# The last chunk's dispatch of an expert-routed transformer kernel: two groups of four row transfers, or four groups of two

## The reference

```
h_flat = (style-modulated norm of x).reshape(2048, 256)
probs = softmax(h_flat @ router_w)            # 8 experts
gates, idx = top_k(probs, 2); gates /= gates.sum(-1)
hid  = relu(h_flat @ exp_w1[e] + exp_b1[e])   # 256 -> 1024
eout = hid @ exp_w2[e] + exp_b2[e]            # 1024 -> 256
out  = x + sum over the two experts of gate * eout
```

## Time and profile before

| | us |
|---|---|
| runs, median of 3 (lowest to highest) | 653.52 (652.57 to 654.47) |
| profiled execution, its own time | 655.13 |
| its span | 653.3 |
| granted TensorE clock, mean | 0.949 |
| TensorE busy | 585.7 |
| VectorE busy | 458.3 |
| ScalarE busy | 308.5 |
| POOL busy | 223.4 |

### The profile page before, as it was taken

One profiled execution on the slowest core, in us unless ns is written; L12 is line 12 of the kernel. 1 busy time (PEld: TensorE's weight loads), 2 busy tenths in 40 slices (PEclk: granted clock), 3 DMA queues, 4 the chain that ended last, 5 costly groups with the idle time before them and its releaser, 6 DMA issues.

```text
span 653.3 us, 15487 instructions
## 1 busy us (share of the span) xinstructions
PE 585.7 (90%) x5008; PEld 422.1 (65%) x5008; DVE 458.3 (70%) x1282; ACT 308.5 (47%) x643; POOL 223.4 (34%) x137
## 2 busy tenths in 40 slices
PE   3979989899878999859987799999899999999995
PEld 1537575476665585844857447778677877777773
DVE  5755995789977879781898752988555656666663
ACT  2418446545373436564343241767456444444442
POOL 3140615047417067043380240222542223323123
PEclk9978899899997999979997699999899999999999
DMA  7995009513285450665605595774533222222320
GB/s 209 321 240 171 3 18 256 190 45 114 68 182 178 138 179 2 171 152 194 206 22 193 219 330 217 270 261 97 140 91 58 44 47 45 45 38 41 58 40 12
DMA packets 41189, 86.58 MB, mean 133 GB/s; under 512 B 7321, under 2 KB 31938, under 8 KB 37026
## 3 DMA queue, kind: packets, MB, share of 16 engines
q1 hardware_dynamic: 21248, 56.47, 25.3%
q0 software_dynamic: 8352, 16.99, 14.1%
q10 hardware_dynamic: 11522, 12.20, 6.2%
HBM read 57.10 MB, written 29.44 MB: 132 GB/s over the span
## 4 chain that ended last, share of the span: by engine, by line
PE 60%; DVE 19%; ACT 7%; DMA 5%; issue 5%; POOL 2%; ACTq 1%; another core or an unknown queue 1%; SPq 0%; POOLq 0%; DVEq 0%
PE bank L1959 10%; PE bank L1768 6%; PE bank L1948 6%; PE bank L1950 5%; PE bank L1949 5%; PE bank L1960 5%; PE bank L1777 4%; DMA stage<-in_moe_w 4%; PE bank L1667 3%; PE bank L1732 2%; PE bank L1748 2%; PE bank L1626 2%; ACT split L685 2%; DVE sc_sum L1155 2%; DVE stats L1075 1%
## 5 line engine op out<-in xcount | busy, mean ns | idle before, releaser
L1950 PE MATMUL bank<-xs_f,w_moe 128*128 128x128 f16 x624 | 122.9, 221 | 2.4 <-issue 2.4
L1948 PE MATMUL bank<-xs_f,w_moe 128*128 128x128 f16 x624 | 122.8, 221 | 2.0 <-DVE xs_f L1520 0.9
L1949 PE MATMUL bank<-xs_f,w_moe 128*128 128x128 f16 x624 | 122.4, 220 | 0.5 <-issue 0.5
L906 ACT ACTIVATE stage<-bank,cols 128x128 f32<-128x128 f32 x312 | 88.9, 370 | 62.7 <-PE bank L1950 26.9
L646 POOL DMA_INDIRECT out_x<-x_kept,ids x39 | 62.6, 1605 | 159.5 <-DVE x_kept L1534 117.8
L1948 PEld LDWEIGHTS bank<-xs_f,w_moe 128*128 x624 | 61.3, 98 | 37.3 <-issue 8.1
L1959 PE MATMUL bank<-w_moe,split 128*128 x208 | 79.5, 384 | 0.6
L1768 PE MATMUL bank<-w_moe 128*128 128x512 f32 x128 | 60.8, 636 | 5.3 <-ACT w_moe L755 5.3
L1042 DVE SCALAR_TENSOR_TENSOR split<-stage,split 128x2048 f16<-128x2048 f32 x16 | 40.2, 2514 | 35.7 <-ACT split L685 35.7
L1949 PEld LDWEIGHTS bank<-xs_f,w_moe 128*128 x624 | 61.5, 99 | 4.0 <-issue 0.9
L558 POOL TENSOR_TENSOR w_moe<-w_moe,sc_max 128x2048 f32<-128x2048 f32 x8 | 29.0, 3622 | 99.1 <-DVE sc_max L1150 99.1
(11 more groups left out here) (271 smaller groups left out, 1196.7 us busy)
## 6 DMA issues: line engine op xcount, KB each, us to landing
stage<-in_moe_w SPq DMA_DIRECT2D x16, 1024.0 KB, 7.9
w_split<-split SPq DMA_DIRECT2D x16, 1024.0 KB
w_moe<-w_split SPq DMA_DIRECT2D x8, 2048.0 KB
w_moe<-in_bias POOLq DMA_DIRECT2D x8, 1024.0 KB, 9.1
xs<-dispatched ACTq DMA_DIRECT2D x41, 130.0 KB
w_moe<-in_x_f SPq DMA_DIRECT2D x4, 512.0 KB, 7.2
w_moe<-in_x_t SPq DMA_DIRECT2D x4, 512.0 KB, 8.0
out_x<-x4b ACTq DMA_DIRECT2D x4, 512.0 KB
```

The costliest lines, as they stand in the source:

```text
L906: ins = act.activation(h32[j][:, f, :], bank[banks + g][:, P * (f % 4):P * (f % 4) + P], ACT.Relu, bias=moe_b1[:, bass.ds(e, 1), f], scale ...
L1948: pe.matmul(o, hi, xs_f[j][:, k, :], start=(k == 0), stop=False)
L1949: pe.matmul(o, hi, xs_f[j][:, KD + k, :], start=False, stop=False)
L1950: mm = pe.matmul(o, lo, xs_f[j][:, k, :], start=False, stop=(k == KD - 1))
```

## The change

POOL's order around the last chunk's dispatch is written anew. In place of transfers for groups 0 and 1, add 6, transfers for groups 2 and 3, add 7, and `confirm`, it runs the two transfers of one group and one add, four times (adds 6 to 9), and `confirm` behind the last add. The adds behind it start at 10 instead of 8. Buffers and semaphores of each add are the same as before (9's `i % 2` and `i % STEPS` give what n gave).

```diff
@@ -655,12 +655,11 @@
             pool.wait_ge(x_stored.sem, x_stored.of(NCH - 1, 0))
             for n in range(6):
                 add_rows(n, n % 2, n % STEPS)
-            dispatch(NCH - 1, range(0, 2))
-            add_rows(6, 0, 0)
-            dispatch(NCH - 1, range(2, TT))
-            add_rows(7, 1, 1)
+            for i in range(TT):
+                dispatch(NCH - 1, range(i, i + 1))
+                add_rows(6 + i, i % 2, i % STEPS)
             confirm(NCH)
-            for n in range(8, EARLY):
+            for n in range(6 + TT, EARLY):
                 add_rows(n, n % 2, n % STEPS)
             pool.wait_ge(x_stored.sem, x_stored.of(NCH, 0))
             with pool.Fori(0, TURNS - EARLY_TURNS) as i:
```

## The result

The changed kernel takes 656.70 us (median of 7 runs, 655.09 to 658.09), the kernel before 652.95 beside it: ratio 1.0054, 95% interval 1.0035 to 1.0073, **3.7 us slower** (2.3 to 4.8 by the interval). The forecast was +3.8.

A forecast was written before the change was run, and what follows sets the result against it. TensorE bounds the kernel, with 8.0 us lost near the dispatch. Stalls 0, later confirmation +1.1 and lowered clock +2.7 sum to +3.8 us on the 653.52 median: 657.3 us, range 652.8 to 661.2.

The forecast's parts named there:

- Steps A to C: POOL's dispatch: pair 2.56 us, waited add 4.79, last add to confirmation 4.4; confirmation, ScalarE's gate at step 12, at 490.4.
- Step D: ScalarE's wait to TensorE's data: 0.41 + 1.75 + 0.1 us, step 13 at 492.7 instead of 491.62, +1.1 us.
- Step E: TensorE's stalls near the dispatch: 8.0 us gained if pairs remove them, then waited off before step 13, worth 0.
- Step F: TensorE's clock behind the 9.1 us pause before step 13: lowered, costing +2.7 us, bounds 0 and 5.2.
- Step G: The other waits, such as VectorE's outputs for adds two tiles back: all satisfied in time, costing nothing.
- Rivals 2 and 3: Stalls near the dispatch: first stays (+6.1 us, 659.6, chance 0.18); both stay, from other traffic (+7.7, 661.2, 0.14).
- Rival 1: Gate costs only itself: some stall stays behind each pair, clock holds; +1.1 us, 654.6, chance 0.14.
- Rival 4: POOL's adds land faster behind pairs, 3.72 us for 4.79: 650.3, or 653.0 with the clock lost; chance 0.12.

The follow-up runs named there:

- e7: The kernel before with four more indirect row transfers on POOL behind add 11, into a table nobody reads, on chip B; 645.56 us, run once.
- e2: The changed kernel, but ScalarE waits at step 12 for the transfers' own semaphore instead of POOL's confirmation; 653.51 us, ratio 1.0005 to the kernel before.
- e10: The changed kernel itself run again, on the same chip as e9; 657.49 us, ratio 1.0086 to the kernel before.
- e4: The kernel before with SP's empty rows held until add 7 has landed and the store of x4b moved from step 9 to step 11; 656.28 us, ratio 1.0041.
- e5: The changed kernel's pairs started one add earlier, ahead of add 5, without confirmation, ScalarE waiting for the transfers themselves; 653.13 us, ratio 1.0107 to the kernel before.
- e9: Pairs issued between an add's issue and its wait, adds 5 to 8, no confirmation, ScalarE waiting for the transfers; 646.40 us, ratio 0.9916 to the kernel before.
- e12: The same program as e7 (the kernel before with four extra row transfers behind add 11), on chip D; 656.08 us, run once.
- e1: The kernel before with only the confirmation moved, behind add 9, the groups of four transfers kept; 656.36 us, ratio 1.0040.

## Why the prediction was right

The time (657.3 for 656.7), the sign and the main mechanism held: the confirmation, two waited adds later, became the bound, and what TensorE gained before it was waited off. One term of the sum, the clock, was much too large, and another a little too small. Step by step:

- **Steps A to C, the gate's time.** 29.05 us from the first transfer to the confirmation were forecast. The load at 490.55 less 0.41 gives 490.1, 29.96 us behind 460.18. Pairs took 2.6 as said (one 2.7), the waited adds 5.23, 5.42 and 4.86 instead of 4.79 each, the last 4.0 instead of 4.4. So it was 0.9 us longer; that this execution reached the dispatch 1.2 us earlier hid it in the absolute times.
- **Step D** held: 1.75 us from the load to the end of the four activations (490.55 to 492.30), and 0.34 instead of 0.1 more to TensorE.
- **Step E**: the gain was to be 8.0 us, worth nothing on the path. Of the 8.0, pairs left 0.95 + 1.40 + 0.82 = 3.2; with the gate 1.1 later against step 9's turn, the pause was 6.9 and not 9.1 us. (The 5.65 us behind both figures is a little off: against e7's steps the kernel before lost 7.5 and the changed one 2.7.) Worth nothing, as said; e2 shows it, where with the gate 3 us earlier the time comes back.
- **Step F** was mis-sized: 2.7 us for the lowered clock. Behind the restart at 492.64 the windows lack 1.36 x 0.5 + 3 x 0.22 = 1.3 us; the clock was lowered in the pause already (0.58 in 488 to 491) and back at 1.00 from 497. And not even the 1.3 reach the end. From step 13's first matmul to the third turn behind it the kernel before takes 15.41 us (491.62 to 507.03) and the changed kernel 15.66, 0.25 more: before, two of these turns are 6.21 and 5.80 us apart, in the changed kernel 5.50 and 5.58. The prediction shifted the end one for one; for the clock that did not hold. In e10 the same stretch takes 16.80 us, so there the clock costs 1.4.

```profile
501.23 0.39 PE L1935 MATMUL bank<-ident,xs 128*128 128x128 f16 x4
...
507.03 0.39 PE L1935 MATMUL bank<-ident,xs 128*128 128x128 f16 x4
```

- **Step G** held: no wait of VectorE for POOL's adds in 455 to 500.

By the two traces the sum is, from step 9's turn to step 13's first matmul, 29.37 us against 27.19: +2.2, and 0.25 behind it: +2.4, at the low end of what the medians allow (2.3 to 4.8). The two profiled executions agree with that: 656.41 and 655.13 us are 1.3 apart, though the changed one had been 1.2 ahead at step 9's turn. In e10 the same sum, against the same rows, is 2.8 + 1.4 = +4.2. Two errors, the gate 1.1 too short and the clock 1.3 to 2.4 too long, cancel in part; that the forecast came within 0.6 us is luck.

Rivals 2 and 3 (the disturbance stays) are refuted by the after trace and e4. Rival 1 was right that some of the stall stays behind each pair and, in the first trace, that the clock costs next to nothing; but the clock did fall, and its 654.6 is 2.1 us under the measured time. Rival 4: the adds landed slower, not faster; POOL went on 4.9 to 5.4 us behind each, not sooner than in the earlier trace rows. The Trainium skill ("DMA: Bandwidth & Descriptors", section "Anatomy of one DMA — SWDGE (gpsimd) path") puts such a transfer at about 2.0 us plus its bytes at 436 GB/s. As an estimate from that page an add would take 2.3 us; the trace has 4.0 for the last one, so it does not agree for the adds. What the prediction did not see at all is that the 8.0 us depend on the chip. On chip B the change was not run; with the gate near 490 it should cost far more there, which e5's 1.0107 (gate at 484.6) makes likely but does not show.

## What to carry to other kernels

Before spreading work out to relieve one engine, look for who waits for its end: a completion that stands behind further waited operations moves by all of them. Where an engine waits for a transfer to land, that wait is the place for the work to be spread (e9), and the consumer's wait should be for the data's own semaphore, not for a message behind another add. A stall that costs 8 us on one chip and nothing on the next asks for runs on several. And a lowered clock is not priced by its windows alone: look whether the steps behind it take back what it cost.

## What was not expected of the hardware

- The same program took 645.2 us on one chip (single runs 642.4 to 650.7) and 651.9 to 654.3 on three others. The traces put the difference into the stalls of the earlier trace rows; TensorE is busy for 29.57 us of the dispatch's 30 in e7 and 24.37 in e12, which are one program. Each chip was used in one sitting only, so the runs can't tell the chip from the hour.
- On the disturbing chips TensorE's matmuls stop around a burst of POOL's row transfers, and other engines wait for matmuls that read as long issued: up to 5.2 us in e12, for five indirect transfers in a row, and up to 6.0 in the earlier trace rows. Against e7's steps, a group of four and its add costs 3 to 5 us on average (before, e1, e4, e12), a pair ahead of its add about 1 (changed kernel, e10), and a pair behind its add's issue nothing (e9). No run shows why; e4 excludes the store and the empty rows, e12 the stretch of the program, nothing more.
- A waited add took 4.8 to 6.7 us until POOL went on (4.79 in the earlier trace rows, 5.42 in the changed kernel, 6.3 and 6.7 in e5). What sets this stays open.
